# Decay factors of a state-space layer: running products on VectorE, or exponentials of differences on GpSimd and ScalarE

## The reference

```
# layer 0: attention over the 1024 tokens
h = group_norm(x, 8 groups)
q, k, v = split(h @ qkv_w.T + qkv_b)
x = x + (softmax(q @ k.T / sqrt(128)) @ v) @ proj_w.T + proj_b

# layer 1: a Mamba-2 layer on the tokens of that x
u = layer_norm(x)
z, xBC, dt = split(u @ in_w.T);  dt = softplus(dt + dt_bias)
xs, B, C = split(silu(causal_conv4(xBC)))
for each token t, each of 4 heads:
    state = state * exp(dt_t * A) + (dt_t * xs_t) outer B_t
    y_t   = state @ C_t
y = (y + D * xs) * silu(z);  y = y / rms(y) * rms_w
out = y @ out_w.T
x + out * sigmoid(se2(relu(se1(mean of out over tokens))))
```

## Time and profile before

| | us |
|---|---|
| median of 3 runs | 271.45 |
| lowest, highest | 271.21, 271.54 |
| the profiled execution | 272.0 |
| its span, first to last instruction | 269.8 |

### The profile page before, as it was taken

How to read it: one execution, slowest core, us unless ns; L and a number is a source line. 1 busy time by engine, 2 the same in 40 slices (tenths; PEclk the granted TensorE clock), 3 DMA queues, 4 the chain that set the end, 5 groups by cost and what they waited for, 6 DMA issues and landing times. The chain is left out here.

```text
span 269.8 us, 6198 instructions
## 1 busy us (share of the span) xinstructions
PE 254.5 (94%) x1992; PEld 224.3 (83%) x1992; DVE 223.4 (83%) x516; ACT 208.1 (77%) x414; POOL 115.8 (43%) x114
## 2 busy tenths in 40 slices
PE   2999999999999999999999999999999999989791
PEld 2989997998899889988899789888988798777680
DVE  4689746565598498999999999999989999799933
ACT  2347577989999875898887799767988889998361
POOL 8010021206402730235289742572286269758440
PEclk9999999999999999999999999999999999999997
DMA  6930000000040340000133300051005100101103
GB/s 177 395 145 4 0 0 4 2 0 0 11 149 5 108 129 2 0 2 0 38 125 112 126 2 0 6 173 64 0 2 193 45 4 2 39 0 42 39 4 117
DMA packets 10987, 15.29 MB, mean 57 GB/s; under 512 B 1515, under 2 KB 5708, under 8 KB 10956
## 3 DMA queue, kind: packets, MB, share of 16 engines
q1 hardware_dynamic: 10412, 14.69, 16.2%
q10 hardware_dynamic: 544, 0.21, 0.3%
HBM read 12.70 MB, written 2.20 MB: 55 GB/s over the span
## 5 line engine op out<-in xcount | busy, mean ns | idle before, releaser
L1169 PE MATMUL attn_out<-values,pT 128*128 128x129 f32 x512 | 65.6, 275 | 0.1
L1169 PEld LDWEIGHTS attn_out<-values,pT 128*128 128x128 f32 x512 | 62.6, 191 | 3.6 <-issue 1.7
L986 DVE TENSOR_REDUCE neg_max<-scores 128x1 f32<-128x1024 f32 x32 | 39.0, 1219 | 16.1 <-PE scores L1169 16.0
L655 ACT ACTIVATE probs<-scores,neg_max 128x512 f32<-128x512 f32 x64 | 42.4, 684 | 9.1 <-DVE neg_max L986 9.0
L661 ACT ACTIVATE pT<-bank 128x512 f32<-128x512 f32 x64 | 37.6, 594 | 14.0 <-PE bank L1247 13.9
L1247 PE MATMUL bank<-ident,probs 128*128 128x128 f32 x256 | 37.7, 273 | 0.0
L1247 PEld LDWEIGHTS bank<-ident,probs 128*128 128x128 f32 x256 | 30.3, 141 | 4.5 <-issue 1.4
L1169 PE MATMUL scores<-h_hi,q_hi 128*128 128x512 f32 x64 | 31.7, 496 | 0.0
L567 POOL TENSOR_TENSOR ln_rstd<-ln_var,neg_half 128x4 f32<-128x4 f32 x8 | 11.3, 1412 | 45.5 <-DVE ln_var L1008 45.5
L1079 DVE TENSOR_TENSOR_SCAN L<-L,ident 128x512 f32<-128x512 f32 x24 | 30.4, 1274 | 0.0
L581 POOL TENSOR_TENSOR pre<-pre,th 128x512 f32<-128x512 f32 x16 | 22.6, 1410 | 15.1 <-ACT pre L687 8.2
(11 more groups left out here) (219 smaller groups left out, 597.2 us busy)
## 6 DMA issues: line engine op xcount, KB each, us to landing
L<-decay_rows_d SPq DMA_DIRECT2D x24, 256.0 KB, 3.8
res<-in_x_tok SPq DMA_DIRECT2D x4, 512.0 KB, 7.9
out<-res SPq DMA_DIRECT2D x8, 256.0 KB, 2.0
x_all<-in_x SPq DMA_DIRECT2D x3, 512.0 KB, 8.6
decay_in<-decay_rows_d SPq DMA_DIRECT2D x24, 64.0 KB, 3.4
x_all<-in_x SPq DMA_DIRECT2D x2, 256.0 KB, 3.2
winT<-in_in_wT SPq DMA_DIRECT2D x1, 194.0 KB, 7.1
wqkv<-in_qkv_w ACTq DMA_DIRECT2D x1, 192.0 KB, 4.0
```

The costliest lines, as they stand in the source:

```text
L655: act.activation(probs[:, i % 2, half_of(h)], scores[:, half_of(h)], ACT.Exp, bias=neg_max[:, i:i + 1]).then_inc(exp_done.sem, 1)
L986: V.tensor_reduce(neg_max[:, n:n + 1], scores[:, :], AX.X, ALU.max, negate=True).then_inc(max_ready.sem, 1)
L1169: return T.matmul(o, w, v, start=start, stop=stop)
```

## The change

For batches a, b and c the rows that go through DRAM are no longer the decays but the sums of their logs, taken from the result of Cum. dA now is a scaled copy of that result for all batches. L is then made in three instructions for each chunk where there was one: two on GpSimd in the new step ld (the spread sums minus the partition's own sum, in place, then plus a mask that is 0 on and above the diagonal and very negative below it), and one on ScalarE, the new form of step l, an exponential in place. VectorE's scan, the tile ident4 and the column first are gone. ld waits for the DMA of its chunk, for dA and for the mask; dA waits until the batch before has had its ld steps; l waits for ld. The weights wqkv now lie in the tile zv, which is first written later. ORDER is a new table throughout. The rest is untouched.

```diff
...
@@ -178,7 +178,6 @@
         pool_banks = [ctx.enter_context(nc.psum_tensor(f"bank{k}", [P, HALF], F32)) for k in range(5)]
 
         ident = sb("ident", [P, P])
-        ident4 = sb("ident4", [P, HEADS, P])
         center = sb("center", [P, P])
         group_avg = sb("group_avg", [P, P])
         upto = sb("upto", [P, P])
@@ -193,7 +192,6 @@
 
         res = sb("res", [P, BATCH, TILES, P])
         vec = sb("vec", [P, VECS])
-        wqkv = sb("wqkv", [P, 3, P])
         wpT = sb("wpT", [P, P])
         ob_row = sb("ob_row", [P, P])
         winT = sb("winT", [P, INPROJ])
@@ -249,6 +247,8 @@
         C0 = sb("C0", [P, TOKENS])
         gate = sb("gate", [P, TOKENS])
         zv = sb("zv", [P, TOKENS])
+
+        wqkv = zv[:, 0:3 * P].rearrange("p (k c) -> p k c", k=3)
         dtx = sb("dtx", [P, 2, R])
         dta = sb("dta", [P, 2, R])
         dte = sb("dte", [P, 2, R])
@@ -265,8 +265,6 @@
         la = sb("la", [P, 2, R])
 
         dA = sb("dA", [P, 2, P])
-
-        first = sb("first", [P, 1])
 
         decay_rows = sb("decay_rows", [2 * R, 2, P])
         rows_d = nc.dram_tensor("decay_rows_d", [BATCH - 1, 2, 2 * R, P], F32).ap()
@@ -350,6 +348,7 @@
         spread = [signal(f"spread{c}", 16) for c in range(TILES)]
         decay_in_ready = [signal(f"decay_in{n}", 16 * HEADS) for n in range(2)]
         cd_ready, decay_ready, l_ready = signal("cd_ready", 2), signal("decay_ready", 2), signal("l_ready", 8)
+        ld_step, ld_ready = signal("ld_step", 8), signal("ld_ready", 8)
         l_last, dA_all_ready, below_ready = signal("l_last", 8), signal("dA_all_ready", 2), signal("below_ready")
         xdt_ready, to_end_ready, xend_ready = signal("xdt_ready", 2), signal("to_end_ready", 2), signal("xend_ready", 2)
         BT_ready, M_ready = signal("BT_ready", 2), signal("M_ready", 8)
@@ -380,7 +379,7 @@
             if kind == "InZ":
                 return [(zt_ready, b, n + 1), (zv_ready, b, n + 1)]
             if kind == "Cum":
-                return [(dec_ready, b, n + 1), (cd_ready, b, n + 1)] + ([] if by_dma(b) else [(dA_ready, b, n + 1)])
+                return [(dec_ready, b, n + 1), (cd_ready, b, n + 1), (dA_ready, b, n + 1)]
             if kind == "DAT":
                 return [(rows_ready, b, n + 1) if by_dma(b) else (dA_T_ready, 0, n + 1)]
             if kind == "G":
@@ -580,6 +579,17 @@
                     wait(pool, tap0["bc"], b, n + 1)
                     pool.tensor_tensor(pre[:, 1, half_of(n)], pre[:, 1, half_of(n)], term(b, n, j), ALU.add
                                        ).then_inc(tap["bc"].sem, 1)
+                elif kind == "ld":
+                    wait(pool, spread[n], b, 16)
+                    wait(pool, dA_ready, b, n // QUAD + 1)
+                    pool.wait_ge(below_ready.sem, 1)
+                    chunk = L[:, HEADS * n:HEADS * (n + 1), :]
+                    c = n % QUAD
+                    pool.tensor_tensor(chunk, chunk, dA[:, n // QUAD, HEADS * c:HEADS * (c + 1)].unsqueeze(2)
+                                       .broadcast_to([P, HEADS, P]), ALU.subtract).then_inc(ld_step.sem, 1)
+                    wait(pool, ld_step, b, n + 1)
+                    pool.tensor_tensor(chunk, chunk, below[:, :].bitcast(F32).unsqueeze(1).broadcast_to([P, HEADS, P]), ALU.add
+                                       ).then_inc(ld_ready.sem, 1)
                 elif kind == "xend":
                     rows = slice(R * n, R * (n + 1))
                     wait(pool, xdt_ready, b, n + 1)
@@ -730,16 +740,11 @@
                     wait(act, dta_ready, b, n + 1)
                     act.activation(dte[:, n, :], dta[:, n, :], ACT.Exp, scale=-1.0).then_inc(dte_ready.sem, 1)
                 elif kind == "dA":
-                    wait(act, sp_step, b, SP_STEPS * (n + 1))
                     act.wait_ge(zeros_done.sem, 5)
                     wait(act, filled["DAT"], b - 1, n + 1)
-                    if by_dma(b):
-                        act.activation(dA[:, n, 0:R], la[:, n, :], ACT.Exp, bias=first[:, :], scale=1.0 / A_SCALE
-                                       ).then_inc(dA_ready.sem, 1)
-                    else:
-
-                        bank = take(act, b, "Cum", n)
-                        act.activation(dA[:, n, 0:R], bank[:, 0:R], ACT.Copy, scale=1.0 / A_SCALE).then_inc(dA_ready.sem, 1)
+                    wait(act, ld_ready, b - 1, QUAD * (n + 1))
+                    bank = take(act, b, "Cum", n)
+                    act.activation(dA[:, n, 0:R], bank[:, 0:R], ACT.Copy, scale=1.0 / A_SCALE).then_inc(dA_ready.sem, 1)
                 elif kind == "dec":
 
                     bank = take(act, b, "Cum", n)
@@ -754,7 +759,11 @@
                                    bank[:, R:2 * R].rearrange("s (c h) -> s h c", h=HEADS)[:, :, chunks]
                                    .unsqueeze(2).broadcast_to([P, HEADS, HEADDIM, QUAD - 1]),
                                    ACT.Exp, scale=1.0 / A_SCALE).then_inc(cd_ready.sem, 1)
-                elif kind == "l" and not by_dma(b):
+                elif kind == "l" and by_dma(b):
+                    wait(act, ld_ready, b, n + 1)
+                    chunk = L[:, HEADS * n:HEADS * (n + 1), :]
+                    act.activation(chunk, chunk, ACT.Exp).then_inc(l_ready.sem, 1)
+                elif kind == "l":
 
                     bank = take(act, b, "L", n)
                     wait(act, filled["Y"], b - 1, n // QUAD + 1)
@@ -866,8 +875,6 @@
                 b0, b1 = (0, 1) if n == 0 else (1, BATCH)
                 if kind == "masks" and n == 0:
                     dve.wait_ge(consts_done.sem, 1)
-                    for h in range(HEADS):
-                        V.tensor_copy(ident4[:, h, :], ident[:, :])
                     step_done(V.tensor_scalar(center[:, :], ident[:, :], 1.0 / P, None, ALU.subtract))
                 elif kind == "masks":
                     dve.wait_ge(consts_done.sem, 1)
@@ -878,7 +885,6 @@
                     step_done(last)
                     V.tensor_copy(pick_chunk[:, :], row_chunk[:, 0, :])
                     V.tensor_copy(head_sel[:, :, :], row_head[:, 1, :].unsqueeze(2).broadcast_to([P, HEADS, HEADDIM]))
-                    V.tensor_scalar(first[:, :], ident[:, 0:1], FIRST_BIAS, None, ALU.mult)
                     step_done(V.tensor_tensor(head_mask[:, :, :], row_head[:, 0, :].unsqueeze(2).broadcast_to([P, HEADS, P]),
                                               row_chunk[:, 1, :].unsqueeze(2).broadcast_to([P, HEADS, P]), ALU.add))
                 elif kind == "gn_stats":
@@ -1072,12 +1078,6 @@
                     V.tensor_tensor(xdt[:, rows, :], bank[:, :].rearrange("p (a b) -> p a b", b=HEADDIM),
                                     dt[:, n, :].unsqueeze(2).broadcast_to([P, R, HEADDIM]), ALU.mult
                                     ).then_inc(xdt_ready.sem, 1)
-                elif kind == "l" and by_dma(b):
-
-                    chunk = L[:, HEADS * n:HEADS * (n + 1), :].rearrange("p a b -> p (a b)")
-                    wait(dve, spread[n], b, 16)
-                    V.tensor_tensor_scan(chunk, chunk, ident4[:, :, :].rearrange("p a b -> p (a b)"), 0.0, ALU.mult, ALU.add
-                                         ).then_inc(l_ready.sem, 1)
                 elif kind == "to_end":
                     rows = slice(R * n, R * (n + 1))
                     if by_dma(b):
```

142 lines of the change are left out of this document (71 added, 71 removed).

## The result

| | before | after |
|---|---|---|
| median, us | 271.5 | 276.27 |
| lowest, highest | 271.21, 272.03 | 275.99, 277.16 |
| the profiled execution, its span | 272.0, 269.8 | 276.52, 274.8 |

The ratio is 1.0167, with a 95% interval from 1.0129 to 1.0204. The time lies in the predicted range and on the predicted side, but the loss is nearly five times the 1.0 us that was forecast, and the time is almost that of the rival in which GpSimd falls behind (276.5). That mechanism is not the one at work: before 236 us TensorE waits for no result of GpSimd, as the rows show.

What follows compares the result with a forecast made beforehand. TensorE was taken to bound the kernel until 230 us. Terms -1.0 + 1.0 + 0.5 + 0.6 = +1.1 gave 273.1 us for the profiled execution, 272.5 for the median; range 268.8 to 277, likeliest case 272.0 to 274.5.

Steps and rivals of the forecast that it cites:

- GpSimd falls behind: Rival: pairs of 2.82 us make xend, h_lo and the powers late in the second half; 276.5 us, chance 0.18.
- the relief 1.0 us: Until 230 us: of at most 2.2 us of TensorE waits, VectorE's freer queue wins back 1.0.
- the fourth of the part on sums: GpSimd and VectorE slow each other: VectorE might get 5 us back of the 30 lost; nothing put in the sum.
- The part of the prediction on the Trainium skill: Shared SBUF interfaces: without the scans, 24 pairs on GpSimd would cost nearer 57 us than 60.
- Queues, +1.0 (0 to 4): Until 230 us: GpSimd's in-order queue and ScalarE's new exponentials leave little spare time; 1.0 us lost together.
- ln_rstd, +0.5: After the last attention product: GpSimd reaches ln_rstd between 1.5 us too early and 2 too late; +0.5 (0 to 3).
- InZ0d, +0.8: This product now stands ahead of the last attention product and makes that 0.8 us later.
- The end, +0.6: The last xend comes 0.6 us later than before, InZ0d's 0.8 included; nothing changes from there to the last store.
- its own two terms, 2.5 and 1.75: Near the end: L7d ends about 2.5 us later, of which VectorE's earlier readiness for to_end hides 1.75.
- the 1.05 us at the transpose: The last transpose of the decays comes 1.05 us later relative to the last attention product: 0.9 queues, 0.15 softplus chain.
- The relief did not reach the end: Rival: pairs of 2.3 to 2.4 us, no late power, 1.5 to 2 us of waits won; 270.1 us, chance 0.30.
- the 3 us that the text allowed: Sign that the forecast is right: TensorE's idle time before 230 us stays under 3 us.

Runs made afterwards that it cites:

- both narrow: Changed kernel with both ld instructions on one column of each head and the 24 exponentials on 4 elements a partition: 271.07 us.
- the split pairs: Changed kernel with each ld instruction on GpSimd cut in four of 128 elements a partition, same result and data moved: 281.10 us.
- narrow pairs: Changed kernel with both ld instructions on 4 elements a partition in place of 512, order, waits and exponentials untouched: 273.48 us.
- a busy GpSimd queue: Changed kernel with each of the 48 ld instructions replaced by a GpSimd power of 4 elements a partition into a scratch tile: 274.34 us.
- the one with res first: Changed kernel with sp14 and sp15 of batch b placed behind res3c and conv_x1c behind res6c: 275.14 us.

## Why the prediction was right in sign and wrong in size

- **The bound.** That TensorE sets the time and never waited for VectorE before 230 was right, and so was "a microsecond taken from VectorE is worth nothing unless TensorE waited for it". The sum then gave the relief 1.0 us all the same. The scans made narrow show none (271.91 against 271.34, with the room that its interval leaves), and the order, the relief and the waits together give 0.3 to 0.4 (271.07 with both narrow).
- **Durations.** A pair is 1.082 + 1.362 = 2.44 us (forecast 2.5), GpSimd 168.5 (176), ScalarE 217.8 (224; an exponential is 0.628, not 0.684). VectorE is 218.9, forecast 195.
- **The step that failed** is the fourth of the part on sums: "If 60 us more on GpSimd lengthened the 61 taps, gates and the like that VectorE reads from SBUF twice by a tenth, VectorE would get 5 us back of the 30 it lost. I put nothing in the sum for it, since VectorE then still has 70 us to spare." The hold was a term of the sum put at nothing. For the 61 instructions that it names the 5 us were near: their durations add up to 48.1 us before and 52.1 after (gates rose from 0.679 to 0.870 us, the taps fell from 0.884 to 0.845). What it left out is the rest: the 80 small instructions of the softplus, most of them of 16 columns, went from 19.8 to 37.5 us, and 15.7 us of VectorE's busy time come back by the pairs alone. The form was wrong as well: an instruction is not lengthened by a share, it stands until GpSimd's ends, so in proportion the smallest are hit most. And spare time in the mean is no cover: res stands in line behind the held step, and TensorE behind res. In time the sum had 0 for this. The runs show 1.9 us for the traffic and 2.8 for the pairs in all (4.9 without the exponentials).
- **The rule that bore on it.** The part of the prediction on the Trainium skill took the GPSIMD Engine Reference's remark as a matter of a few us on GpSimd. GpSimd got them in part: the taps of B and C fell from 1.410 to 1.293 us, while its gating product xs rose from 1.406 to 1.536. The Trainium skill's page SBUF — State Buffer (section "SBUF: two separate sides") says that whichever of the two engines starts first has the shared pair of ports for its whole instruction while the other fully blocks. The rows at 132.71 and 132.89, and the split pairs, agree with it. GpSimd's powers do not: they read SBUF too and last 1.0 us, and nothing is held beside them, so for them the measurement decides. Read with the durations of the pairs, the rule would have turned the "tenth" into a wait of up to 1.3 us for each of the small steps.
- **Queues, +1.0 (0 to 4).** Both causes named there were real: on the path at the end of this section ScalarE's exponentials cost 2.4 and GpSimd's fuller queue 0.9, 3.3 together, inside the 0 to 4. I took the low side. The place was another than the text had: with narrow pairs TensorE waits 1.5 us for ScalarE's stateT and not for probs or pT. They do not simply add to the hold: with everything wide the exponentials cost 0.25.
- **ln_rstd, +0.5.** It waits 0.36 us for VectorE and starts 1.65 us behind the end of the last product, 1.74 before. The text named that as the sign that the power is not late: nothing.
- **InZ0d, +0.8.** It is part of the +0.6 of the next item. Not a cost: put back, it costs 1.9.
- **The end, +0.6.** The transpose comes 15.5 us behind the product, inside the 15 to 17 (14.8 before); the last xend 23.5 behind it, and 23.8 before. Without InZ0d's 0.8 the text's 0.6 has that xend 0.2 nearer to the product, so this came as forecast (its own two terms, 2.5 and 1.75, leave 0.75 and not 0.6). The chain from product to end takes 44.7 us, and 44.6 before. So 0.8 of the 1.05 us at the transpose came, and all of it was hidden behind the transpose.
- **The rivals.** The time is that of "GpSimd falls behind", and the mechanism is not. Its threshold, a pair of 2.65 us, was not reached by the mean pair of 2.44; the cut pairs at 3.7 us show what it looks like (281.1 us). The relief did not reach the end, and TensorE's idle time before 230 us, 4.1, is over the 3 us that the text allowed.
- **The range.** 276.27 lies inside 268.8 to 277, but outside the likeliest case (272.0 to 274.5), and it got there with luck: the upper end was made of 4 us of queues and 3 at the power. The queues gave up to 3.3, the power nothing, and the hold, which had no term, filled the place.

From the kernel before to the changed one the runs make one path: order and relief -0.4 (271.07), exponentials +2.4 (273.48), a busy GpSimd queue +0.9 (274.34), its traffic +1.9 (276.27). On another path the pairs come first with 4.9 and the exponentials last with 0.25. Only the sum is independent of the way. What is still open is how the 4.9 of this second path divides between traffic and queue, since powers with narrow exponentials were not run. No variant that computes everything beat the kernel before; the best of the changed form is the one with res first, 275.14 us.

## What to carry to other kernels

Work on GpSimd that streams SBUF tiles is not free for VectorE even when GpSimd has the time: price each GpSimd instruction as a possible wait of its whole length for the small VectorE instruction behind which something critical stands, and keep such steps, and the read that frees a PSUM bank, away from it. An engine at 83% that nobody waits for is not a bound, and relieving it gave nothing here that could be measured. To price parts of a change that comes with a new order, keep the order and make the instructions narrow; swapping order and instructions against each other measures only that they belong together.
